# MLP third layer two periods late beside the first layer; pixels and channels turned in 64-row tiles

## The chip, the cores and the metric

One Trainium2 chip, one of its cores. The metric is the device time in microseconds (us) of one execution. The engines are called PE (TensorE), DVE (VectorE), ACT (ScalarE), POOL (GpSimd) and SP (SyncE, which here only issues DMAs).

## The reference

Two layers run over x of shape 8 x 512 x 32 x 32, that is 8 images of 512 channels and 1024 pixels.

```python
x = x + _L0_conv_ref(_gn(x), ...)   # group norm, 8-head attention over 1024 pixels, output projection
x = x + _L1_conv_ref(_gn(x), ...)   # windowed deformable attention, below
```

The second layer normalises over channels, cuts the image into 16 windows of 8 x 8 pixels and, for each of 8 groups of 64 channels, finds 4 sample points in a window, takes keys and values there, and lets each pixel attend to the 4 points of its window. To the similarities a bias is added, made by a small MLP from the distance of pixel and point:

```python
mu = x.mean(axis=1, keepdims=True)
xn = (x - mu) / jnp.sqrt(var + 1e-06) * ln_w[None, :, None, None] + ln_b[None, :, None, None]
q = jnp.einsum('bgihw,goi->bgohw', xg, wq)
...
bias = jnp.sign(pos) * jnp.log1p(jnp.abs(pos))        # 2 numbers per pair of pixel and point
bias = jax.nn.relu(bias @ cpb_w1.T + cpb_b1)          # 2 -> 128, the first layer
bias = jax.nn.relu(bias @ cpb_w2.T + cpb_b2)          # 128 -> 128, the second layer
bias = bias @ cpb_w3.T + cpb_b3                       # 128 -> 1, the third layer
```

The MLP runs over 8 groups x 16 windows x 4 points x 64 pixels per image.

## The kernel before, in words

**Order.** Each engine has its own program, with the order written out by hand and semaphores between the engines. The loop runs over the images i = 0..7. An image's turn is 32 steps of attention (first layer of the reference), the output projection (L603), the group norm and the windowing of the result, and then the **MLP stage**: `mlp(i - 1, i)` computes the MLP of the image before, and beside it the channel norm of image i. The MLP of image 7 runs alone at the end (`i is None`). So there are 8 MLPs; 7 of them carry the norm of an image. Image 0 has its norm without an MLP.

**The MLP.** It has 32 units (u = 0..31) in 16 pairs (v = 0..15). For a unit, PE makes the first layer with two matmuls over tiles of 32 rows (`mlp1_unit`, L833; a pair gives four matmuls that run beside each other). ACT takes the relu as the high half (`relu1`, L1118), DVE the low half (`low1`, L1567). The second layer is three matmuls of 128 x 128 x 512 for each half unit (`mlp2(u, w)`, L852 to L854, into three banks that go round). ACT empties one half unit of each unit (L1134), DVE the other (L1583), into `H2`, a ring of 4 units. The third layer (`mlp3(v)`, L862) takes a pair of units in tiles of 32 columns, 8 instructions, all summed into one bank `OB`. The PE order of one pair, here called a period, is written out in L884 to L891:

```python
for v in range(1, WIN):
    if v + 1 < WIN:
        mlp1(v + 1)
    mlp2(2 * v, 0)
    mlp2(2 * v, 1)
    mlp2(2 * v + 1, 0)
    mlp3(v - 1)
    mlp2(2 * v + 1, 1)
```

`mlp1(v + 1)` waits until DVE has emptied both first-layer slots; `mlp2(u, 0)` waits for `low1(u)`; each `mlp2` waits until the bank of three half units earlier is empty; ACT and DVE wait with unit u until `mlp3` of the units in its ring place is done.

**The norm beside it.** At the MLP's start PE turns the normalised image from channel rows to pixel rows (`pixels(n)`, n = 0..3, L806, 8 transposes of 128 x 128 each, two banks per n; n even is emptied by ACT at L1124, n odd by DVE at L1437). DVE takes statistics of the 8 pixel tiles (`row_stats`, L1444) after units 0 to 7, their means after unit 9 (`row_means`, L1448 to L1452) and the shifts after unit 12; ACT normalises the 8 tiles in place (L1107) after units 14 to 21. At the end PE turns them back (`channel(t)`, t = 0..3, L817, 8 transposes each): `channel(0)` stands between the last second layer and `mlp3(15)`, the other three behind it. Channel tiles are emptied with the affine scale: t = 0, 2 by DVE (`affine`, L1461), t = 1, 3 by ACT (L1272), out of two slots in turn. Then follow the transposes of the bias (L901) and `queries` (L825, 16 matmuls). For image 0 the same operations use the ring slots (L1260 and L1763 empty the pixels).

**A DMA beside it.** Before the stage, `point_outputs` are kept by ACT in a place that the high halves of units 2 and 3 share. So `relu1(2)` waits (`ms_out`) until SP's DMA has taken them to DRAM.

**Elsewhere.** The attention turns its exponentials with transposes of 64 rows (`turn`, L660: 16 of them, the two row halves into two banks), and L1079 and L1398 empty these with a pattern that puts the halves together.

## Time and profile before

| what | us |
|---|---|
| median of 3 runs | 3103.03 |
| lowest, highest | 3098.18, 3104.87 |
| the profiled execution's own time | 3095.78 |
| its span, first to last instruction | 3094.0 |

The page gives, for each engine, its busy time and share of the span, and the chain of work that ended last. The mean granted clock of PE was 0.966 of full. In the timelines each line is a start, a duration, an engine, a line of the kernel, the operation and its tiles, and in brackets the idle time of the engine before it and what ended that. A matmul's duration includes its passage through the array, so the cost of one in a stream is read from start to start.

### The profile page before, as it was taken

Reading aid. Unit: us, or ns where it says so; the run is one execution under the profiler, and the core shown is the slowest. Engines: PE = TensorE matmul, PEld = TensorE weight load, DVE = VectorE, ACT = ScalarE, POOL = GpSimd, SP = SyncE. Lnnn points to the kernel's source line nnn. Section 1 sums busy time; section 2 is a strip of 40 time slices with the busy share of each in tenths; the row PEclk is TensorE's granted clock in tenths of the full one; section 3 lists DMA queues with packets and bytes.
Section 4 is the critical chain, followed back from the end, with each engine's and each line's share of the span. In section 5 each row is a group of like instructions: output and inputs, shape, how many; then the busy total and the mean of one; then the engine's idle time right before and its main releaser. Section 6 shows DMA issues by size and latency. Waiting matters only on the chain.

```text
span 3094.0 us, 59663 instructions
## 1 busy us (share of the span) xinstructions
PE 2826.2 (91%) x24696; PEld 1964.6 (63%) x24696; DVE 2207.2 (71%) x2934; ACT 1657.7 (54%) x2429; POOL 197.0 (6%) x157
## 2 busy tenths in 40 slices
PE   6999799999999999899999999999998999998858
PEld 5666576756766577665776667665676756765434
DVE  5666677687775787767867777668777587775746
ACT  2563465374663755535654556536465375663624
POOL 0000020000200002000020001100020000200200
PEclk9999899999999999999999999999999999998968
DMA  5123013311134011340123211332113311104040
GB/s 196 51 59 110 28 33 90 116 58 52 37 80 165 6 54 37 102 145 28 37 62 119 93 42 32 64 123 79 44 38 86 121 51 52 37 12 169 14 105 28
DMA packets 141534, 221.10 MB, mean 71 GB/s; under 512 B 77713, under 2 KB 96660, under 8 KB 137396
## 3 DMA queue, kind: packets, MB, share of 16 engines
q1 hardware_dynamic: 136596, 190.03, 19.8%
q10 hardware_dynamic: 4672, 27.26, 3.6%
q8 instruction: 199, 3.26, 0.7%
q14 instruction: 67, 0.55, 0.1%
HBM read 162.40 MB, written 54.84 MB: 70 GB/s over the span
## 4 chain that ended last, share of the span: by engine, by line
PE 71%; DVE 16%; issue 4%; DMA 3%; ACT 3%; SPq 1%; another core or an unknown queue 0%; ACTq 0%; DVEq 0%; POOL 0%
PE banks L673 12%; PE banks L613 10%; PE banks L642 9%; PE banks L660 8%; PE banks L603 6%; PE banks L852 5%; PE banks L715 4%; PE banks L862 3%; DVE neg_max L1389 3%; PE banks L853 3%; PE banks L854 3%; DVE exps_turned L1398 3%; DMA point_outputs_dram<-point_outputs 2%; PE banks L825 2%; DVE qk_halves L1567 1%
## 5 line engine op out<-in xcount | busy, mean ns | idle before, releaser
L1389 DVE TENSOR_REDUCE neg_max<-banks 128x1 f32<-128x1024 f32 x512 | 601.4, 1216 | 91.1 <-PE banks L642 90.3
L1069 ACT ACTIVATE exps<-banks,neg_max 128x1024 f32<-128x1024 f32 x512 | 566.6, 1113 | 46.7 <-DVE neg_max L1389 46.5
L1079 ACT ACTIVATE exps_turned<-banks 128x1024 f32<-128x1024 f32 x256 | 262.3, 1025 | 579.8 <-PE banks L660 569.4
L1398 DVE COPY exps_turned<-banks 128x1024 f32<-128x1024 f32 x256 | 313.1, 1223 | 324.7 <-PE banks L660 310.5
L642 PE MATMUL banks<-qk_halves 64*128 64x512 f32 x3072 | 440.3, 418 | 72.1 <-ACT exps L1069 49.2
L673 PE MATMUL banks<-exps_turned,values 128*64 128x256 f32 x4096 | 480.0, 384 | 0.8 <-issue 0.8
L660 PEld LDWEIGHTS banks<-ident,exps 64*128 64x128 f32 x8192 | 312.1, 140 | 215.4 <-issue 190.1
L660 PE MATMUL banks<-ident,exps 64*128 64x64 f32 x8192 | 367.4, 229 | 43.8 <-DVE exps_turned L1398 38.7
L642 PEld LDWEIGHTS banks<-qk_halves 64*128 64x128 f32 x3072 | 296.9, 192 | 124.4 <-issue 88.7
L673 PEld LDWEIGHTS banks<-exps_turned,values 128*64 128x64 f32 x4096 | 279.7, 137 | 138.3 <-issue 4.0
L1567 DVE SCALAR_TENSOR_TENSOR qk_halves<-banks,qk_halves 128x1024 fp32r<-128x1024 f32 x256 | 301.6, 1217 | 85.6 <-ACT qk_halves L1118 85.4
L613 PE MATMUL banks<-x_hi,wqk_ring 128*128 128x512 f32 x992 | 340.0, 406 | 0.0
L1118 ACT ACTIVATE qk_halves<-banks 128x1024 fp32r<-128x1024 f32 x256 | 249.2, 1023 | 147.5 <-PE banks L833 128.2
L852 PE MATMUL banks<-qk_halves,mlp_w_hi 128*128 128x512 f32 x512 | 233.1, 455 | 28.4 <-ACT exps L1134 21.6
L613 PEld LDWEIGHTS banks<-x_hi,wqk_ring 128*128 128x128 f32 x992 | 188.5, 190 | 44.5
L1583 DVE TENSOR_SCALAR exps<-banks,mlp_b 128x512 f32<-128x512 f32 x256 | 189.9, 745 | 31.9 <-PE banks L854 24.8
L852 PEld LDWEIGHTS banks<-qk_halves,mlp_w_hi 128*128 128x128 f32 x512 | 98.3, 192 | 177.3 <-ACT exps L1134 125.6
L853 PE MATMUL banks<-qk_halves,mlp_w_hi 128*128 128x512 f32 x512 | 205.2, 401 | 0.0
L854 PE MATMUL banks<-qk_halves,mlp_w_lo 128*128 128x512 f32 x512 | 204.3, 399 | 0.0
L613 PE MATMUL banks<-x_lo,wqk_ring 128*128 128x512 f32 x496 | 195.5, 394 | 0.0
L715 PE MATMUL banks<-wv_halves,x_hi 128*128 128x512 f32 x512 | 168.8, 411 | 18.4 <-DVE x_lo L1360 18.4
L1134 ACT ACTIVATE exps<-banks,mlp_b 128x512 f32<-128x512 f32 x256 | 168.4, 693 | 28.9 <-PE banks L854 28.4
(181 smaller groups left out, 3344.2 us busy)
## 6 DMA issues: line engine op xcount, KB each, us to landing
wqk_ring<-wqk_split SPq DMA_DIRECT2D x62, 512.0 KB, 4.3
wo_halves<-wo_split_dram SPq DMA_DIRECT2D x8, 2048.0 KB, 7.6
exps_turned<-in_x SPq DMA_DIRECT2D x32, 512.0 KB, 5.5
x_dram<-exps SPq DMA_DIRECT2D x32, 512.0 KB, 2.6
exps_turned<-x_dram SPq DMA_DIRECT2D x32, 512.0 KB, 6.2
out<-exps_turned SPq DMA_DIRECT2D x32, 512.0 KB, 2.8
recips_b<-recips_dram SPq DMA_DIRECT2D x240, 64.0 KB, 3.5
x_image<-in_x ACTq DMA_DIRECT2D x14, 1024.0 KB, 14.2
```

What stands on the lines that cost most here:

```text
L613: mm = pe.matmul(dst, weights[:, a, k], half[:, k, c:c + 512], start=(k == 0 and a == 0 and half is XH), stop=(k == CT - 1 and a == 1))
L642: mm = pe.matmul(slot(("s", 2 * n + h, i))[:, 512 * c:512 * c + 512], QK[rows, p % 2, a, P * j:P * j + P], QK[rows, p % 2, b, 512 * c:512 ...
L660: mm = pe.transpose(TB[:, r, kt * D:kt * D + D], PB[rows, 2 * h + n % 2, kt * P:(kt + 1) * P], IDENT[rows, rows])
L673: mm = pe.matmul(OB[D * h:D * h + D, 0:256], V[:, kt, hc:hc + D], PT[:, u % 2, h, kt], start=(kt == 0), stop=(kt == KT - 1))
L715: mm = pe.matmul(slot(("v", n, i))[:, 512 * s:512 * s + 512], half[:, k, P * tt:P * tt + P], WV[:, a, k], start=(k == 0 and half is XH and ...
L852: pe.matmul(h2_bank(c), W2H[:], h1_hi_half(u)[:, cols], start=True, stop=False)
L853: pe.matmul(h2_bank(c), W2H[:], h1_lo_half(u)[:, cols], start=False, stop=False)
L854: pe.matmul(h2_bank(c), W2L[:], h1_hi_half(u)[:, cols], start=False, stop=True)\
L1069: freed(act.activation(PB[:, 2 * h + n % 2], slot(("s", m, i)), ACT.Exp, bias=NM[:, m:m + 1], accum_out=SS[:, m:m + 1]), ("s", m, i))
L1389: dve.tensor_reduce(NM[:, m:m + 1], slot(("s", m, i)), AX.X, ALU.max, negate=True).then_inc(mx, 1)
L1398: dve.tensor_copy(PT[:, n // 2 % 2, 1, :, P * j:P * j + P].rearrange("p k (r q) -> p k r q", r=2), TB.rearrange("p r (k q) -> p k r q", k= ...
L1567: freed(dve.scalar_tensor_tensor(out=h1_lo_half(u), in0=slot(("h1", u, j)), scalar=0.0, in1=h1_hi_half(u).bitcast(F32), op0=ALU.max, op1=A ...
```

## The change

The third layer now comes two periods late: `mlp3(v - 2)` directly behind `mlp1(v + 1)`, ahead of the four `mlp2` of the period, which follow each other without a break. `mlp3(14)` stands behind the last `mlp2`, ahead of `channel(0)`. For that, `H2` becomes a ring of 6 units: the two new ones, `H2X`, lie in free space behind `window_outputs`. DVE's statistics go from units 0 to 7 to the even units 0 to 14, the means to unit 16 and the shifts to unit 18, ACT's normalising to units 21 to 28. The transposes of pixels and channels are made as 16 of 64 rows in place of 8 of 128 rows, the upper and lower row halves into two banks, and the six lines that empty them put the halves together by their access pattern. No instruction is added or removed on ACT, DVE, POOL or SP.

```diff
+        H2X = at("mlp_hidden_more", [P, 2, HW], AT_PT + 8192)
...
+        def h2_unit(u):
+            return H2[:, u % 6] if u % 6 < 4 else H2X[:, u % 6 - 4]
+
+        def pixel_halves(ap):
+            return ap.rearrange("p b (t r c) -> p (b t) r c", t=CT, r=2)
+
+        def from_halves(ap):
+            return ap.rearrange("p (r x c) -> p x r c", r=2, c=D)
+
+        def channel_halves(t):
+            return A[:, t].rearrange("p (x r c) -> p x r c", r=2, c=D)
...
@@ pixels(n, i), 8 of 128 rows become 16 of 64 rows
-                        mm = pe.transpose(dst[:, 512 * s + P * t:512 * s + P * (t + 1)],
-                                          A[:, t, P * (2 * n + s):P * (2 * n + s + 1)], IDENT[:])
+                        for r in range(2):
+                            rows = slice(D * r, D * r + D)
+                            c0 = 512 * r + D * (CT * s + t)
+                            mm = pe.transpose(dst[:, c0:c0 + D], A[rows, t, P * (2 * n + s):P * (2 * n + s + 1)],
+                                              IDENT[rows, rows])
@@ channel(t, i)
-                    mm = pe.transpose(slot(("tc", t, i))[:, P * r:P * (r + 1)], XP[:, r, P * t:P * (t + 1)], IDENT[:])
+                    for h in range(2):
+                        rows = slice(D * h, D * h + D)
+                        c0 = 512 * h + D * r
+                        mm = pe.transpose(slot(("tc", t, i))[:, c0:c0 + D], XP[rows, r, P * t:P * (t + 1)],
+                                          IDENT[rows, rows])
@@ mlp3(v)
-                                       H2[:, (2 * v + s // 2) % 4, 512 * (s % 2):512 * (s % 2) + 512],
+                                       h2_unit(2 * v + s // 2)[:, 512 * (s % 2):512 * (s % 2) + 512],
@@ mlp(j, i), PE
-                    mlp2(2 * v, 0)
-                    mlp2(2 * v, 1)
-                    mlp2(2 * v + 1, 0)
-                    mlp3(v - 1)
-                    mlp2(2 * v + 1, 1)
+                    if v >= 2:
+                        mlp3(v - 2)
+                    for u in (2 * v, 2 * v + 1):
+                        for w in range(2):
+                            mlp2(u, w)
+                mlp3(WIN - 2)
                 if i is not None:
                     channel(0, i)
                 mlp3(WIN - 1)
@@ mlp(j, i), ACT
-                        act.activation(XP[:, 4 * n:4 * n + 2].rearrange("p b c -> p (b c)"), TB_ALL,
+                        act.activation(pixel_halves(XP[:, 4 * n:4 * n + 2]), from_halves(TB_ALL),
...
-                    if u >= 4:
-                        act.wait_ge(l3_done, j * WIN + u // 2 - 1)
-                    act.activation(H2[:, u % 4, 0:512], h2_bank(2 * u), ACT.Relu, bias=B2[:, 0:1])\
+                    if u >= 6:
+                        act.wait_ge(l3_done, j * WIN + u // 2 - 2)
+                    act.activation(h2_unit(u)[:, 0:512], h2_bank(2 * u), ACT.Relu, bias=B2[:, 0:1])\
                         .then_inc(h2_done[0], 1)
-                    if i is not None and 14 <= u < 22:
-                        normalise_rows(u - 14, i)
+                    if i is not None and 21 <= u < 29:
+                        normalise_rows(u - 21, i)
@@ mlp(j, i), DVE: the ring's waits as on ACT, and
-                        if u < PXT:
-                            ins = row_stats(u, i)
-                            if u == PXT - 1:
+                        if u < 2 * PXT and u % 2 == 0:
+                            ins = row_stats(u // 2, i)
+                            if u == 2 * PXT - 2:
                                 after = mark(ins)
-                        if u == PXT + 1:
+                        if u == 2 * PXT:
                             row_means(after)
-                        if u == PXT + 4:
+                        if u == 2 * PXT + 2:
                             row_shifts(i)
```

The other lines that empty pixels (L1260, L1437, L1763) and channels (L1272, L1461) get the same patterns.

## Rows read from the trace of the kernel before

**Rows 1.** The page, its parts 1 and 4: engines, and the chain by engine.

```profile
PE 2826.2 (91%) x24696; PEld 1964.6 (63%) x24696; DVE 2207.2 (71%) x2934; ACT 1657.7 (54%) x2429; POOL 197.0 (6%) x157
...
PE 71%; DVE 16%; issue 4%; DMA 3%; ACT 3%; SPq 1%; another core or an unknown queue 0%; ACTq 0%; DVEq 0%; POOL 0%
```

**Rows 2.** Timeline of PE, one period (start us, duration us, ..., [idle before <-releaser]).

```profile
1051.52 0.39 PE L833 MATMUL banks<-attended,mlp_w_rows 21*128 21x512 bf16 x4
1051.85 0.50 PE L852 MATMUL banks<-qk_halves,mlp_w_hi 128*128 128x512 f32 x1
1052.18 0.40 PE L853 MATMUL banks<-qk_halves,mlp_w_hi 128*128 128x512 f32 x1
...
1053.79 0.39 PE L854 MATMUL banks<-qk_halves,mlp_w_lo 128*128 128x512 f32 x1
1054.11 1.07 PE L862 MATMUL banks<-exps,mlp_w_slide 128*32 128x512 f32 x8
1055.11 0.50 PE L852 MATMUL banks<-qk_halves,mlp_w_hi 128*128 128x512 f32 x1
...
1056.00 0.39 PE L833 MATMUL banks<-attended,mlp_w_rows 21*128 21x512 bf16 x4
```

**Rows 3.** The same timeline, DVE, the same period.

```profile
1053.01 2.36 DVE L1567 SCALAR_TENSOR_TENSOR qk_halves<-banks,qk_halves 128x1024 fp32r<-128x1024 f32 x2 [0.63 <-ACT qk_halves L1118]
```

**Rows 4.** Timeline of DVE where it never stops, earlier in this MLP.

```profile
1016.68 0.68 DVE L1444 BATCH_NORM_STATS2 ln_bn<-pixels 128x6 f32<-128x512 f32 x1
1017.28 2.34 DVE L1567 SCALAR_TENSOR_TENSOR qk_halves<-banks,qk_halves 128x1024 fp32r<-128x1024 f32 x2
1019.53 1.41 DVE L1583 TENSOR_SCALAR exps<-banks,mlp_b 128x512 f32<-128x512 f32 x2
1020.86 0.18 DVE L1450 BATCH_NORM_AGGREGATE ln_mean_var<-ln_bn 128x2 f32<-128x6 f32 x1
```

**Rows 5.** Timeline of ACT in a period with two L1107 rows.

```profile
1038.47 1.94 ACT L1118 ACTIVATE qk_halves<-banks 128x1024 fp32r<-128x1024 f32 x2
```

**Rows 6.** Timeline of PE: starts of L833 in three periods following each other.

```profile
1015.20 0.39 PE L833 MATMUL banks<-attended,mlp_w_rows 21*128 21x512 bf16 x4
...
1019.82 0.40 PE L833 MATMUL banks<-attended,mlp_w_rows 21*128 21x512 bf16 x4
...
1024.59 0.40 PE L833 MATMUL banks<-attended,mlp_w_rows 21*128 21x512 bf16 x4
```

**Rows 7.** Timeline of PE at the end of the last MLP.

```profile
3069.56 1.07 PE L862 MATMUL banks<-exps,mlp_w_slide 128*32 128x512 f32 x8 [0.94 <-DVE exps L1583]
```

**Rows 8.** Timeline of PE in the attention: transposes of 64 rows, and what follows.

```profile
1110.87 0.71 PE L660 MATMUL banks<-ident,exps 64*128 64x64 f32 x16
1111.39 0.94 PE L642 MATMUL banks<-qk_halves 64*128 64x512 f32 x6
```

**Rows 9.** Timeline of the channel stage behind an MLP.

```profile
1069.16 1.04 PE L817 MATMUL banks<-ident,pixels 128*128 128x128 f32 x8
...
1072.38 1.20 ACT L1272 ACTIVATE normed<-banks,ln_b_T,ln_w_T 128x1024 f32<-128x1024 f32 x1 [0.32 <-PE banks L817]
...
1073.73 1.07 PE L817 MATMUL banks<-ident,pixels 128*128 128x128 f32 x8 [0.51 <-ACT normed L1272]
...
1075.07 1.45 PE L825 MATMUL banks<-normed,wq_blocks 128*128 128x512 f32 x3
```

**Rows 10.** The page, part 5: the copy out of two banks with a pattern.

```profile
L1079 ACT ACTIVATE exps_turned<-banks 128x1024 f32<-128x1024 f32 x256 | 262.3, 1025 | 579.8 <-PE banks L660 569.4
```

**Rows 11.** Waits of L1118 (ACT): until, us in total, times.

```profile
  DMA point_outputs_dram<-point_outputs: 19.1, 5
```

**Rows 12.** Timeline of the first image: its channel stage.

```profile
338.83 6.37 PE L817 MATMUL banks<-ident,pixels 128*128 128x128 f32 x32 [6.15 <-DVE qk_halves L1373]
```

**Rows 13.** Windows: length, busy of PE PEld DVE ACT POOL, PEclk, DMA, GB/s.

```profile
1071.30:1075.10 3.80, 3.29 (x32) 3.08 (x30) 1.62 (x2) 2.15 (x3) 0.00 (x0) 1.00 0.00 0
...
999.70:1002.70 3.00, 3.00 (x10) 1.60 (x9) 3.00 (x5) 1.50 (x3) 0.00 (x0) 0.50 0.83 333
```

More of the change, by code:

```diff
@@ L1259, in _ @@
                     wait_full(act, ("tp", n, i))
-                    freed(act.activation(XP[:, 2 * n:2 * n + 2].rearrange("p b c -> p (b c)"), slot(("tp", n, i)),
+                    freed(act.activation(pixel_halves(XP[:, 2 * n:2 * n + 2]), from_halves(slot(("tp", n, i))),
                                          ACT.Copy), ("tp", n, i))
@@ L1271, in _ @@
                     wait_full(act, ("tc", t, i))
-                    freed(act.activation(A[:, t], slot(("tc", t, i)), ACT.Identity, scale=LNWT[:, t:t + 1],
+                    freed(act.activation(channel_halves(t), from_halves(slot(("tc", t, i))), ACT.Identity, scale=LNWT[:, t:t + 1],
                                          bias=LNBT[:, t:t + 1]), ("tc", t, i))
@@ L1436, in pixel_rows @@
                 dve.wait_ge(tpx_full[1], 2 * (i - 1) + n // 2 + 1)
-                dve.tensor_copy(XP[:, 2 * n:2 * n + 2].rearrange("p b c -> p (b c)"), OM_ALL).then_inc(tpx_done[1], 1)
+                dve.tensor_copy(pixel_halves(XP[:, 2 * n:2 * n + 2]), from_halves(OM_ALL)).then_inc(tpx_done[1], 1)
             def row_stats(r, i):
@@ L1460, in affine @@
                 wait_full(dve, ("tc", t, i))
-                freed(dve.tensor_scalar(A[:, t], slot(("tc", t, i)), LNWT[:, t:t + 1], LNBT[:, t:t + 1], ALU.mult, ALU.add),
+                freed(dve.tensor_scalar(channel_halves(t), from_halves(slot(("tc", t, i))), LNWT[:, t:t + 1],
+                                        LNBT[:, t:t + 1], ALU.mult, ALU.add),
                       ("tc", t, i))
@@ L1580, in mlp @@
                     dve.wait_ge(h2_full[1], j * UNITS + u + 1)
-                    if u >= 4:
-                        dve.wait_ge(l3_done, j * WIN + u // 2 - 1)
-                    dve.tensor_scalar(H2[:, u % 4, 512:1024], h2_bank(2 * u + 1), B2[:, 0:1], 0.0, ALU.add, ALU.max)\
+                    if u >= 6:
+                        dve.wait_ge(l3_done, j * WIN + u // 2 - 2)
+                    dve.tensor_scalar(h2_unit(u)[:, 512:1024], h2_bank(2 * u + 1), B2[:, 0:1], 0.0, ALU.add, ALU.max)\
                         .then_inc(h2_done[1], 1)
                     if i is not None:
-                        if u < PXT:
-                            ins = row_stats(u, i)
-                            if u == PXT - 1:
+                        if u < 2 * PXT and u % 2 == 0:
+                            ins = row_stats(u // 2, i)
+                            if u == 2 * PXT - 2:
                                 after = mark(ins)
-                        if u == PXT + 1:
+                        if u == 2 * PXT:
                             row_means(after)
-                        if u == PXT + 4:
+                        if u == 2 * PXT + 2:
                             row_shifts(i)
@@ L1762, in _ @@
                         wait_full(dve, ("tp", n, i))
-                        freed(dve.tensor_copy(XP[:, 2 * n:2 * n + 2].rearrange("p b c -> p (b c)"),
-                                              slot(("tp", n, i))), ("tp", n, i))
+                        freed(dve.tensor_copy(pixel_halves(XP[:, 2 * n:2 * n + 2]),
+                                              from_halves(slot(("tp", n, i)))), ("tp", n, i))
                 if i:
```

## The prediction

> **What bounds the kernel now.** I read the page first: PE is busy for 91% of the span and the chain that ended last runs over PE for 71% and over DVE for 16% [rows 1]. So what counts is time on PE, and the places where PE waits for an emptying engine. Then I read one period of the MLP on PE's timeline [rows 2]. From L833 to the next L833 it is 4.48 us, and PE has no idle time in it. To be seen are the steps from start to start. Inside a run of second-layer matmuls a step is 0.23 (seven of them from 1052.18 to 1053.79). The first matmul of 128 rows behind a tiled block takes 0.33, the last one before a tiled block 0.32, L833 to what follows 0.33, and L862 to what follows 1.00. So each tiled block costs about 0.10 in front and 0.10 behind beyond its own work, and a period has two such blocks. In this period DVE sits idle for 0.63, until ACT's high half is there [rows 3]: PE sets the pace, DVE follows.
>
> **The third layer beside the first.** The new period on PE is L833, L862, then twelve matmuls: 0.33 + 1.00 + 0.33 + 10 x 0.23 + 0.32 = 4.28, that is 0.20 less than 4.48 [rows 2]. This takes the step from the first layer (row tiles) to the third (column tiles) at 0.33, as the step from the first layer to the second; no row shows it. The bounds: it costs nothing (0.10 less) or 0.20 more, so that nothing is gained. I take the middle, since every switch in the rows costs about 0.10. Blocks that merge: v = 2 to 14, 13 per MLP, 8 MLPs: 13 x 8 x 0.20 = **20.8 us**. At v = 15 `mlp3(13)` stands alone as before; `mlp3(14)` no longer splits a run of matmuls, which spares one long first step, 0.1 x 8 = **0.8**. In the last MLP, PE waits 0.94 for DVE ahead of `mlp3(15)` [rows 7]; `mlp3(14)` now fills that: **0.9**.
>
> The Trainium skill, page "TensorEngine Tiling (Array Packing)", section "Key Properties", says that a change of the tiling mode, not of the tile alone, drains the engine. By this the step from first to third layer is a switch as well and the sum stays; without a drain there it would be the 0.10 less per merged block of the first rival. The rows agree for full and tiled blocks (0.10 on each side).
>
> Does anything else stop a period of 4.28? DVE's load with one `row_stats` is 0.60 + 2.25 + 1.33 = 4.18 [rows 4]. Its first `low1` starts 1.49 after L833 [rows 2, 3]; 1.49 + 4.18 = 5.67, and the next may start at 4.28 + 1.49 = 5.77. It fits by 0.10. ACT with two L1107 per period has no idle time at 4.48 [rows 5], so its load is up to 0.20 over the new period, for three periods and one half at each side. That backlog of at most 0.6 first eats the slack of the first-layer slots: DVE's second `low1` ends 1.49 + 2.36 = 3.85 after L833, 0.43 ahead of where PE asks [rows 2, 3]. I take 0 and keep 0.2 x 7 = 1.4 as bound. The waits on the longer ring ask for a third layer two periods old; nothing queues behind them.
>
> **Statistics spread.** Two `row_stats` per period put DVE behind, and the periods after them take 4.62 and 4.77 [rows 6]; over 4.48 that is 0.43. Spread out, DVE keeps up; the means come where no statistics are left. I take 0.3 x 7 = **2.1** (bounds 0 and 3.0). The shifts and the normalising come seven units later; unit 28 is two periods ahead of `channel(0)`, which waits for them: nothing.
>
> **Transposes.** Eight of 128 rows with the four of L901 take 1.34, or 0.11 each, 0.89 for eight [rows 9]. Sixteen of 64 rows that turn as much take 0.52, from 1110.87 to the next start [rows 8]. So one group saves up to 0.4. That the halves run beside each other is shown there, with the same operands.
> In the channel stage: `channel(0)` is ahead of `mlp3(15)` on PE, 0.4. ACT's affine waits 0.32 for `channel(1)`, and then `channel(3)` waits for that affine [rows 9]: shorter transposes take off the 0.32, after which ACT itself is late (its bias row stands ahead). `channel(3)` is shorter by 0.4 itself. With rounding 1.2 of the 4 x 0.4 arrives at `queries` at 1075.07, and behind it PE and DVE follow each other. 1.2 x 7 = **8.4** (bounds 0.4 and 1.6 each, 2.8 and 11.2).
> The emptying lines read two banks side by side. The nearest row is L1079, 1025 ns for 128x1024 [rows 10], beside two L1118 in 1.94 [rows 5]: I take 0. For the affine no row exists; 0.1 each, two on the path, is the bound, 1.4.
> In the pixel stage five of seven MLPs then wait for the DMA of the point outputs, 19.1 us together [rows 11]: what PE gains there goes into that wait. If the DMA were early, 0.4 more each, 2.0. The other two give at most 0.4 each; I take **0.5** in all. In the first image nothing hides the turning, and its 32 transposes take 6.37 [rows 12]: between 1.2 and 3.2; I take 2.0, and 0.8 for its pixels (bounds 0 and 1.6), **2.8**.
>
> **Sum.** 20.8 + 0.8 + 0.9 + 2.1 + 8.4 + 0.5 + 2.8 = 36.3, say 36 us. The profiled execution took 3095.8, so it would be 3059.8. That execution lies 7.3 under the median of 3103.0; for the median I expect **3067**.
>
> **Rivals.** A difference within 0.2% (6 us) can't be told from none here.
> 1. The switch from first to third layer is free. Then the period is 4.18, where DVE's 4.18 is the bound too: 13 x 8 x 0.10 = 10 more, 3057. Against it: no switch in the rows is free. 7%.
> 2. Merging saves nothing, because that switch costs 0.20 more; 36 - 21 = 15, so 3088. For it: row tiles to column tiles is the one switch not in these rows. This is also the case in which the change does not do what it says. 8%.
> 3. DVE becomes the bound of the eight periods with statistics. It fits by 0.10 only. If each period kept the idle 0.63 ahead of `low1` [rows 3], it would be 4.18 + 0.63 = 4.81 there, 8 x 0.53 x 7 = 30 lost, 3097. Against it: that idle time is there because PE is slower than DVE. 5%.
> 4. PE's clock. It fell to 0.50 in a stretch of 3.0 us, in which PE was busy for all of it [rows 13]; at half speed such a stretch costs 1.5. It followed a wait in the MLP's start. Shorter transposes with the same waits leave PE emptier in the channel and pixel stages. One more such stretch per norm, 7 x 1.5 = 10: 3077. Against it: in the channel stage the granted clock stays at 1.00 with 0.51 idle [rows 9, 13]. 10%.
> 5. The same, strong enough to turn the sign. It decides from 36 / 1.5 = 24 more low stretches, over three per image; with four, 42 lost, 3109: slower. 2%.
>
> On 4 and 5: from 1071.30 to 1075.10 nearly all of PE's work is transposes, and the granted clock is 1.00 [rows 13]. The Trainium skill, page "TensorE: Matmul & The Clock Gate", section "Part 4: PE-mode transpose", says that transposes do not count as work for the clock. By that rule shorter transposes could only help the clock, and 4 and 5 would have no chance. The trace disagrees with it, so I keep them.
>
> **The numbers.** The forecast has 68%, its own range with the bounds above 3058 to 3075. The range of 8 in 10 takes in rivals 1, 2 and 4: 3052 to 3088. Faster by over 0.2%: all but rival 5 and part of 3, 95%; same 3%, slower 2%.
>
> **What would show it.** On PE's timeline L833 follows L833 after 4.28, L862 stands 0.33 behind L833, and the runs of twelve have steps of 0.23; with 4.18 or 4.48 rival 1 or 2 is right. With rival 3 the periods of the even units up to 14 are longer than the later ones, with DVE named ahead of L833. The channel stage, from the last L854 to L825, is shorter by 1.2 beyond the moved third layer. Windows show the clock. The prediction is wrong if the periods stay at 4.48, or if ACT's wait for the DMA grows by more than the pixels gave.

## The result, and the profile after

| what, us | before | after |
|---|---|---|
| median, 4 runs each, on the same chip | 3102.02 | 3061.58 |
| lowest, highest | 3098.18, 3104.87 | 3059.65, 3069.95 |
| ratio of the medians, 95% interval | | 0.9876 [0.9853, 0.9898] |
| profiled execution, own time | 3095.78 | 3069.95 |
| its span | 3094.0 | 3068.1 |
| mean granted clock | 0.966 | 0.963 |

The change makes the kernel faster by 40 us (the interval of the ratio is 32 to 46). The execution that was profiled is the slowest of the four of after, 8.4 over the median; its span is only 25.9 shorter than before's. So the traces must be read by stages, and something in this execution gives back a part of the gain. The page first, to compare with [rows 1]:

```profile
PE 2788.4 (91%) x25208; PEld 1956.1 (64%) x25208; DVE 2200.3 (72%) x2934; ACT 1667.9 (54%) x2429; POOL 196.7 (6%) x157
...
PE 74%; DVE 13%; DMA 5%; issue 3%; ACT 3%; SPq 2%; another core or an unknown queue 0%; ACTq 0%; DVEq 0%; POOL 0%
```

PE's busy time went down by 38 and its share of the chain up, at DVE's cost (16% to 13%). The DMA's share went from 3% to 5%: there stands a part of what was given back. The timeline of PE in one period, the answer to [rows 2] (L853 is the first layer, L872 to L874 the second, L882 the third; L1139, L1155, L1128 on ACT are the old L1118, L1134, L1107, and L1589 on DVE the old L1567):

```profile
1033.67 0.39 PE L853 MATMUL banks<-attended,mlp_w_rows 21*128 21x512 bf16 x4
1033.99 1.06 PE L882 MATMUL banks<-mlp_hidden_more,mlp_w_slide 128*32 128x512 f32 x8
1034.99 0.50 PE L872 MATMUL banks<-qk_halves,mlp_w_hi 128*128 128x512 f32 x1
1035.32 0.39 PE L873 MATMUL banks<-qk_halves,mlp_w_hi 128*128 128x512 f32 x1
...
1037.62 0.39 PE L874 MATMUL banks<-qk_halves,mlp_w_lo 128*128 128x512 f32 x1
1037.94 0.39 PE L853 MATMUL banks<-attended,mlp_w_rows 21*128 21x512 bf16 x4
```

L882 stands 0.32 behind L853, then come 1.00, 0.33, ten steps of 0.23 and 0.32: a period is 4.27, and PE never waits. DVE where it has one `row_stats` per period, the answer to [rows 4]:

```profile
1016.07 0.74 DVE L1605 TENSOR_SCALAR mlp_hidden_more<-banks,mlp_b 128x512 f32<-128x512 f32 x1
1016.73 0.68 DVE L1465 BATCH_NORM_STATS2 ln_bn<-pixels 128x6 f32<-128x512 f32 x1
1017.33 0.74 DVE L1605 TENSOR_SCALAR mlp_hidden_more<-banks,mlp_b 128x512 f32<-128x512 f32 x1
1018.07 1.23 DVE L1589 SCALAR_TENSOR_TENSOR qk_halves<-banks,qk_halves 128x1024 fp32r<-128x1024 f32 x1
```

The profile names no idle time here, but the next L853 on PE does not wait for it. From its start the first L1605 takes 0.66 to the next row and the second 0.74; the 0.08 more may be what DVE has left over in a period. ACT in the periods with two L1128, the answer to [rows 5]:

```profile
1038.65 1.93 ACT L1139 ACTIVATE qk_halves<-banks 128x1024 fp32r<-128x1024 f32 x2
...
1043.01 1.95 ACT L1139 ACTIVATE qk_halves<-banks 128x1024 fp32r<-128x1024 f32 x2
...
1047.38 1.98 ACT L1139 ACTIVATE qk_halves<-banks 128x1024 fp32r<-128x1024 f32 x2
```

These are 4.36 and 4.37 apart, with no idle time between: here ACT is the bound. PE's L853 starts at 1042.21, 1046.59 and 1050.97, so two periods of an MLP take 4.38. The channel stage, the answer to [rows 9]:

```profile
1060.20 0.71 PE L836 MATMUL banks<-ident,pixels 64*128 64x64 f32 x16
...
1060.84 1.06 PE L882 MATMUL banks<-exps,mlp_w_slide 128*32 128x512 f32 x8
...
1061.84 1.32 PE L836 MATMUL banks<-ident,pixels 64*128 64x64 f32 x32
...
1062.60 1.20 ACT L1293 ACTIVATE normed<-banks,ln_b_T,ln_w_T 128x1024 f32<-128x1024 f32 x1
...
1063.94 0.71 PE L836 MATMUL banks<-ident,pixels 64*128 64x64 f32 x16 [0.78 <-ACT normed L1293]
...
1065.08 1.45 PE L845 MATMUL banks<-normed,wq_blocks 128*128 128x512 f32 x3
```

From the last third layer, L882 at 1060.84, to the queries at L845 it is 4.24, where before it was 4.81 (L862 to L825, 1075.07). The affine at 1062.60 has no idle time in front of it, where [rows 9] had 0.32; `channel(3)` now waits 0.78 for it instead of 0.51. The block of 16 transposes at 1060.20 takes 0.64 to the next start, where 8 of 128 rows took 1.10 (1069.16 to 1070.26). The end of the last MLP, the answer to [rows 7], and the first image's channel stage, the answer to [rows 12]:

```profile
3042.78 0.39 PE L874 MATMUL banks<-qk_halves,mlp_w_lo 128*128 128x512 f32 x1
3043.10 1.07 PE L882 MATMUL banks<-mlp_hidden_more,mlp_w_slide 128*32 128x512 f32 x8
3044.11 1.06 PE L882 MATMUL banks<-exps,mlp_w_slide 128*32 128x512 f32 x8
3045.97 0.66 PE L922 MATMUL banks<-ident,exps 128*128 128x128 f32 x4 [0.80 <-ACT exps L1162]
```

```profile
334.99 2.31 PE L836 MATMUL banks<-ident,pixels 64*128 64x64 f32 x32 [5.96 <-DVE qk_halves L1394]
337.63 2.17 PE L836 MATMUL banks<-ident,pixels 64*128 64x64 f32 x32 [0.34 <-DVE normed L1482]
340.19 2.08 PE L845 MATMUL banks<-normed,wq_blocks 128*128 128x512 f32 x2 [0.39 <-DVE normed L1482]
```

The 0.94 of waiting is gone: `mlp3(14)` fills it. The last place is the MLP's start. The waits of L1139, the answer to [rows 11], and one of them in the timeline:

```profile
  DMA point_outputs_dram<-point_outputs: 35.9, 7
```

```profile
989.81 1.94 ACT L1139 ACTIVATE qk_halves<-banks 128x1024 fp32r<-128x1024 f32 x2 [5.95 <-DMA point_outputs_dram<-point_outputs]
...
992.38 0.80 PE L872 MATMUL banks<-qk_halves,mlp_w_hi 128*128 128x512 f32 x1 [5.29 <-ACT exps L1155]
...
992.98 0.63 PE L873 MATMUL banks<-qk_halves,mlp_w_hi 128*128 128x512 f32 x1
...
993.40 0.63 PE L874 MATMUL banks<-qk_halves,mlp_w_lo 128*128 128x512 f32 x1
```

All seven MLPs wait there now, for 35.9 in all, where before five waited 19.1. PE runs out of work behind it for 5.29, and its next steps are 0.42 instead of 0.23 (992.98 to 993.40). Last, windows of the channel stage and of this start, the answer to [rows 13]:

```profile
1061.00:1064.70 3.70, 2.92 (x57) 1.90 (x50) 2.65 (x2) 1.83 (x3) 0.00 (x0) 1.00 0.00 0
988.70:998.80 10.10, 6.42 (x17) 4.36 (x18) 7.40 (x9) 5.66 (x8) 0.00 (x0) 0.50 0.78 275
```

The granted clock stays at 1.00 in the channel stage, though PE is busy there for only 2.92 of 3.70. It falls to 0.50 while PE stands idle in the wait for the DMA (its last matmul before is at 986.70), and stays there for the 10.1 us of the second window.

A table by stages shows the whole. It is worked out from the starts of PE's rows in the timeline and summed over the MLPs. The **start** runs from the first L833 (now L853) to that of pair 1, and the **wait** from there to that of pair 2, the stretch with the DMA wait. The **periods** run to `mlp3(15)` and the **channels** from there to the queries. The last MLP is counted apart, and so is the first image, from its projection to its queries. "Low" is the time at the low clock (granted 0.50), over the whole span.

| us | before | after | forecast of the difference |
|---|---|---|---|
| start, 7 MLPs | 51.7 | 51.1 | -0.5 |
| wait, 7 MLPs | 37.7 | 49.5 | 0 |
| periods, 7 MLPs | 488.2 | 464.3 | -23.8 (18.2 + 0.7 + 2.1, and 0.4 x 7 of the channels) |
| channels, 7 MLPs | 33.7 | 29.6 | -5.6 (the other 0.8 x 7) |
| last MLP and its tail | 103.9 | 99.4 | -3.6 (2.6 + 0.1 + 0.9) |
| first image | 65.4 | 63.0 | -2.8 |
| low | 210 | 230 | |

Without the row of the wait the differences make 35.3 (from the unrounded starts), against a forecast of 36.3. The wait gives back 11.8, and the remaining 2.4 of the 25.9 lie outside these stages. Two rows hide something. The start is 0.28 shorter in six MLPs (6.61 to 6.33) and 1.03 longer in the seventh (12.07 to 13.10), which stays unexplained. And the wait costs more than its own row: the first period behind it, from pair 2 to pair 3, is counted in the periods, and its mean granted clock is 0.55 to 0.78 in after, where it was 0.73 to 1.00 in before.

### The profile page after: what moved, and what is told of

It reads as the page before. It is cut to its first block, busy times and chain, and to the rows that moved or that the text cites. A ratio compares the mean times of both kernels' runs of the same rounds, so it can differ in the third digit from the quotient of the medians.

```text
span 3068.1 us, 60655 instructions
## 1 busy us (share of the span) xinstructions
PE 2788.4 (91%) x25208; PEld 1956.1 (64%) x25208; DVE 2200.3 (72%) x2934; ACT 1667.9 (54%) x2429; POOL 196.7 (6%) x157
## 4 chain that ended last, share of the span: by engine, by line
PE 74%; DVE 13%; DMA 5%; issue 3%; ACT 3%; SPq 2%; another core or an unknown queue 0%; ACTq 0%; DVEq 0%; POOL 0%
PE banks L686 12%; PE banks L626 10%; PE banks L655 9%; PE banks L673 9%; PE banks L616 6%; PE banks L872 5%; PE banks L882 4%; PE banks L873 4%; PE banks L874 4%; PE banks L728 4%; DMA point_outputs_dram<-point_outputs 3%; DVE neg_max L1410 3%; DVE exps_turned L1419 3%; PE banks L845 2%; SPq L487 2%
## 5 line engine op out<-in xcount | busy, mean ns | idle before, releaser
L1090 ACT ACTIVATE exps<-banks,neg_max 128x1024 f32<-128x1024 f32 x512 | 566.9, 1114 | 46.2 <-DVE neg_max L1410 46.0
L1589 DVE SCALAR_TENSOR_TENSOR qk_halves<-banks,qk_halves 128x1024 fp32r<-128x1024 f32 x256 | 302.1, 1220 | 89.0 <-ACT qk_halves L1139 88.7
L1139 ACT ACTIVATE qk_halves<-banks 128x1024 fp32r<-128x1024 f32 x256 | 249.7, 1029 | 77.4 <-PE banks L853 41.6
L872 PE MATMUL banks<-qk_halves,mlp_w_hi 128*128 128x512 f32 x512 | 224.5, 438 | 34.0 <-ACT exps L1155 31.6
L873 PE MATMUL banks<-qk_halves,mlp_w_hi 128*128 128x512 f32 x512 | 206.9, 404 | 0.0
L874 PE MATMUL banks<-qk_halves,mlp_w_lo 128*128 128x512 f32 x512 | 206.6, 403 | 0.0
L872 PEld LDWEIGHTS banks<-qk_halves,mlp_w_hi 128*128 128x128 f32 x512 | 100.2, 196 | 157.2 <-issue 99.7
L616 PE MATMUL banks<-attended_hi,wo_halves 128*128 128x512 f32 x512 | 160.0, 394 | 5.5 <-DMA wo_halves<-wo_split_dram 5.5
L1155 ACT ACTIVATE exps<-banks,mlp_b 128x512 f32<-128x512 f32 x176 | 121.8, 698 | 62.8 <-PE banks L874 62.8
## 6 DMA issues: line engine op xcount, KB each, us to landing
x_image<-in_x ACTq DMA_DIRECT2D x14, 1024.0 KB, 10.6
```

The lines of the kernel that those rows point to most:

```text
L616: mm = pe.matmul(dst[:, 512 * n:512 * n + 512], weights[:, a, k, n0:n0 + P], half[:, k, 512 * n:512 * n + 512], start=(k == 0 and a == 0 a ...
L872: pe.matmul(h2_bank(c), W2H[:], h1_hi_half(u)[:, cols], start=True, stop=False)
L873: pe.matmul(h2_bank(c), W2H[:], h1_lo_half(u)[:, cols], start=False, stop=False)
L874: pe.matmul(h2_bank(c), W2L[:], h1_hi_half(u)[:, cols], start=False, stop=True)\
L1090: freed(act.activation(PB[:, 2 * h + n % 2], slot(("s", m, i)), ACT.Exp, bias=NM[:, m:m + 1], accum_out=SS[:, m:m + 1]), ("s", m, i))
L1589: freed(dve.scalar_tensor_tensor(out=h1_lo_half(u), in0=slot(("h1", u, j)), scalar=0.0, in1=h1_hi_half(u).bitcast(F32), op0=ALU.max, op1=A ...
```

## The experiments

All ratios are to the kernel before, run beside the variant on the same chip. Three chips were used. The medians of before on them were 3119.97 (`t_only`, `m_only`, `split3`, `ms_moved`), 3124.42 (`after_again`, `before_ms`, `stats_packed`, `paired3`) and 3107.66 (`ms_again`, `ms_early1`, `pix128`, `ch128`), so the kernels are compared by ratio, and a ratio is turned into microseconds with the median of its chip. Each profile is one execution.

### 1. One half of the change at a time

`t_only` is the kernel before with only the 64-row transposes and the six patterns (the hunks `pixels` and `channel` of the diff, L1260, L1437, L1763, L1272, L1461, L1124). `m_only` is the change without these.

> The kernel before with only the transposes in 64 rows; the MLP's order, ring and statistics stay. If the terms of the sum add up, it is faster than before by 8.4 (channel) + 0.5 (pixels) + 2.8 (first image) = 12 us, ratio 0.996. Rival: the pixels' part goes into the wait for the point outputs' DMA and the channel stage gives only what the trace after shows from mlp3(15) to the queries (4.34 to 3.76, 0.6 per image, and 0.5 ahead of it): then 5 to 8 us. MLP periods stay at 4.48 in both.

> The changed kernel with its transposes put back to 128 rows: only the third layer's place, the ring of six and the spread statistics are left. Theory (terms add): 20.8 + 0.8 + 0.9 + 2.1 = 25 us faster than before, ratio 0.992, periods 4.27. Rival (the transposes carry more than their term, or the DMA wait eats part of this one): under 18 or over 32 us.

Measured: `t_only` 3111.28, 0.9968 [0.9951, 0.9984], a gain of 10. `m_only` 3097.97, 0.9934 [0.9912, 0.9957], a gain of 21. The stages say why neither is larger. In `t_only` the start gains 0.28 in six of the seven MLPs and the channels 0.58 in each; but the wait takes 44.2 where before took 37.7, and the periods 492.6 where before took 488.2. All of the latter is the first period behind the wait: its seven add up to 44.5 against 39.4, at a mean granted clock of 0.62 to 0.75. In `m_only` the periods and the last MLP gain 20.1 and 5.0, which is the expected 25, and the wait gives back 8.5. The two gains add up to 31; with intervals of 5 to 15 and of 13 to 27 that doesn't contradict the 40 of the whole. The interval of `t_only` takes in both its expectation (12) and most of its rival (5 to 8), so the times don't decide between them.

### 2. The third layer late, but not beside the first

Is it the merging that gains, or only that the third layer comes late and the second layer is never waited for? `split3` keeps the six-unit ring and the lateness, and puts the tiled block back where it was:

```diff
-                    if v >= 2:
-                        mlp3(v - 2)
-                    for u in (2 * v, 2 * v + 1):
-                        for w in range(2):
-                            mlp2(u, w)
+                    mlp2(2 * v, 0)
+                    mlp2(2 * v, 1)
+                    mlp2(2 * v + 1, 0)
+                    if v >= 2:
+                        mlp3(v - 2)
+                    mlp2(2 * v + 1, 1)
```

> The changed kernel with the third layer, still two periods late, put back between the third and the fourth second-layer product, away from the first layer. Theory (a tiled block of its own costs 0.10 in front and 0.10 behind): periods go from 4.27 to 4.48, 13 x 8 x 0.2 = 21 us slower than the changed kernel, so 19 us faster than before. Rival (the gain comes from waiting less for the emptying of H2, since the third layer asks for older data, not from merged blocks): periods stay at 4.3 and it is as fast as the changed kernel, 40 us faster than before.

Measured: 3107.25, 0.9960 [0.9944, 0.9975], a gain of 12 (8 to 17) where the whole change has about 40 and 19 were expected. The timeline of PE in one period:

```profile
1063.30 0.40 PE L853 MATMUL banks<-attended,mlp_w_rows 21*128 21x512 bf16 x4
1063.63 0.50 PE L872 MATMUL banks<-qk_halves,mlp_w_hi 128*128 128x512 f32 x1
...
1065.58 0.39 PE L874 MATMUL banks<-qk_halves,mlp_w_lo 128*128 128x512 f32 x1
1065.90 1.06 PE L882 MATMUL banks<-exps,mlp_w_slide 128*32 128x512 f32 x8
1066.90 0.50 PE L872 MATMUL banks<-qk_halves,mlp_w_hi 128*128 128x512 f32 x1
...
1067.79 0.39 PE L853 MATMUL banks<-attended,mlp_w_rows 21*128 21x512 bf16 x4
```

The step from L853 to a full block (0.33), the step into L882 (0.32) and that out of it (1.00 for 8 matmuls) are all as in [rows 2], and the period is 4.49 again; the periods' stage takes 485.2, against 464.3 in after and 466.0 in its repetition (section 3). So the gain is the pair of transitions that the merged block does without. The lateness by itself brings nothing that shows: the periods are 3.0 shorter than in before, and the spread statistics account for that (3.4, see the part on the prediction). The 7 us by which the expectation missed have their like in the wait, whose stage takes 43.9 where before took 37.7.

### 3. The statistics as they were

```diff
-                        if u < 2 * PXT and u % 2 == 0:
-                            ins = row_stats(u // 2, i)
-                            if u == 2 * PXT - 2:
+                        if u < PXT:
+                            ins = row_stats(u, i)
+                            if u == PXT - 1:
@@ the means at PXT + 1 and the shifts at PXT + 4, as before
```

> The changed kernel itself, for its trace a second time and to compare with the others of this call. Theory: 37 to 41 us faster than before, ratio 0.987 to 0.988; the wait of ACT for the point outputs' DMA (35.9 us in the first trace) is the part that moves from execution to execution. Rival: that wait is the same each time, within 3 us.

> The changed kernel with DVE's statistics back behind units 0 to 7, the means behind unit 9, the shifts behind unit 12. Theory (the spread was worth its term): the periods behind the statistics go to 4.6 or more, 2 to 4 us slower than the changed kernel. Rival (at periods of 4.27 a DVE load of 4.8 bites fully, eight units in four periods at 4.8): 4 x 0.5 x 7 = 14 us slower. Second rival: no difference, the early MLP waits anyway.

Measured: `after_again` (the changed kernel once more) 3085.43, 0.9869 [0.9849, 0.9889]; `stats_packed` 3093.10, 0.9905 [0.9892, 0.9918]. Packed statistics cost 8 us by the medians and 11 by the ratios. My expectation of 2 to 4 fell, and the rival's 14 was too much. The periods' stage takes 472.6, against 466.0 in `after_again` and 464.3 in after, 0.9 to 1.2 more per MLP. The six periods from pair 3 to pair 9, where nearly all of the packed statistics stand, are together 7.5 longer in the seven MLPs than in after. PE's timeline, with two `row_stats` per period on DVE:

```profile
2121.79 0.40 PE L853 MATMUL banks<-attended,mlp_w_rows 21*128 21x512 bf16 x4 [0.29 <-DVE qk_halves L1589]
...
2126.55 0.40 PE L853 MATMUL banks<-attended,mlp_w_rows 21*128 21x512 bf16 x4 [0.42 <-DVE qk_halves L1589]
```

These periods are 4.76 long and PE names DVE's L1589 ahead of L853. That is the same length as the worst of before [rows 6]: with two `row_stats` in each period DVE becomes the bound once its slack is used up, whatever PE would do, and in such periods all that the shorter one could bring is lost. The prediction had measured the spread against a period of 4.48; against one of 4.28 it is worth 0.2 more for each such period, and for those in which DVE catches up.

### 4. The wait for the point outputs

`ms_moved` is the change with the point outputs kept elsewhere, in the place of units 4 and 5 of the ring, so that `relu1(2)` waits for nothing; the wait moves to unit 4. `before_ms` moves them to the same place in the kernel before, where no unit of the ring lies, and there the wait stands only ahead of DVE's first copy of turned exponentials of the next image. (`ms_moved` has this wait too, once, in image 1.) And `ms_again` is `ms_moved` once more.

```diff
-        MS = at("point_outputs", [P, CT, C], AT_QK + 24576)
+        MS = at("point_outputs", [P, CT, C], AT_PT + 8192)
...
-                    if u == 2:
-                        act.wait_ge(ms_out, 16 * (j + 2))
@@ ahead of the emptying into unit 4, on ACT and on DVE
+                    if u == 4:
+                        act.wait_ge(ms_out, 16 * (j + 2))
```

> The changed kernel with the buffer of the point outputs moved from the place shared with the high halves of units 2 and 3 into the place of the two new ring units, so that ACT asks for the DMA's landing with unit 4 and not with unit 2. In the trace after, ACT waits for that DMA in all seven MLPs, 35.9 us together. Theory (that wait is on the path since the pixel stage got shorter): from L833 of pair 1 to that of pair 2 it goes from 5.8 to 8.2 down to 4.3, in sum 10 to 20 us faster than the changed kernel. Rival (the rows of the MLP or the emptying engines end next at nearly the same time, or the low clock follows all the same): within 4 us of the changed kernel.

> The kernel before with only the buffer of the point outputs moved to the free place behind window_outputs, and the wait of relu1(2) for it gone; a wait at the next image's first copy guards the buffer. In the trace before, ACT waits 19.1 us for that DMA in five MLPs. Theory (the DMA was on the path in part already): 8 to 14 us faster than before, less than the 14 us between the changed kernel and the same move there. Rival (the wait is new with the change, and before it was covered): within 3 us of before.

> The kernel with the moved buffer a second time, as the base of the next one on the same chip: 50 to 56 us faster than before, ratio 0.982 to 0.984; from L853 of pair 1 to that of pair 2 it takes 4.1 to 4.5 in all seven MLPs with a norm. If instead it is near 0.987, the gain of the move in the first call was chance.

Measured: `ms_moved` 3067.66, 0.9830 [0.9807, 0.9854]; `before_ms` 3107.45, 0.9949 [0.9934, 0.9964]; `ms_again` 3048.67, 0.9823 [0.9803, 0.9843]. In all three no engine waits for this DMA any more, and the stage of the wait takes 29.6 to 30.2, where before takes 37.7 and the two profiles of after 49.5 and 43.9. So the wait was on the path before the change: to take it away is worth 16 there (11 to 21). The stage of the wait explains 7.5 of it in the two profiles; that of before has less waiting than those of the changed kernel, and no second one was taken. In the changed kernel it is worth 12 to 16 (0.9876 and 0.9869 against 0.9830 and 0.9823). Without the wait the change itself is worth 53 - 16 = 37 us, give or take 9 by the two intervals.

The timeline of ACT and PE shows what is left at this place in `ms_moved`:

```profile
995.95 1.94 ACT L1137 ACTIVATE qk_halves<-banks 128x1024 fp32r<-128x1024 f32 x2 [2.43 <-PE banks L853]
...
998.52 0.50 PE L872 MATMUL banks<-qk_halves,mlp_w_hi 128*128 128x512 f32 x1 [1.77 <-ACT exps L1155]
```

ACT now waits 2.43 for PE, because the first layer of pair 1 stands behind six second-layer matmuls, and PE then waits 1.77 for ACT.

### 5. The transposes' places one by one

`pix128` is after with only the pixels turned in 128 rows, `ch128` with only the channels. Each was run once.

> The changed kernel with the pixels alone turned in 128 rows. For its stages only: from the first L853 of an MLP to that of pair 1 it takes 6.6 as before and not 6.3, while the channel stage stays short (3.76 from the last third layer to the queries). Rival (the halves of the channels do the pixels' part too): 6.3.

> The changed kernel with the channels alone turned in 128 rows. From the last third layer to the queries 4.34 as before and not 3.76, and from the third layer of pair 14 to that of pair 15 about 2.1 and not 1.64; the pixel stage stays at 6.3. By the prediction's term the two differences come to 1.2 us per image; the traces so far say 0.58 + 0.43 = 1.0.

Measured: 3055.39 and 3059.50, beside a median of before of 3107.66. One execution each can't rank them, so only their stages are read. Channels: `ch128` takes 33.7 for the channels, as before, and `pix128` 29.6, as after. From the third layer of pair 14 to that of pair 15, with `channel(0)` between, `ch128` takes 2.02 and `pix128` 1.64. A row of `ch128`, as in [rows 9]:

```profile
1065.60 1.07 PE L833 MATMUL banks<-ident,pixels 128*128 128x128 f32 x8 [0.51 <-ACT normed L1289]
```

First image: neither 65.40 (before), pixels alone (`ch128`) 64.69, channels alone (`pix128`) 63.75, both 63.04. By these the pixels are worth 0.71 and the channels 1.65. But two more kernels with neither took 64.60 (`before_ms`) and 64.52 (`m_only`), less than the one with the pixels alone; so the channels are worth 0.8 to 1.65, and a gain of the pixels is shown only beside short channels. Pixels beside an MLP: in `pix128` the start is longer by 1.6 for six MLPs, but the wait takes 39.0 against 49.5 and 43.9, with 4 waits for the DMA of 17.2 in all. That what the pixels gain in front of that wait goes into it is not shown by this: `m_only` has the same pixels, and its wait takes 46.2.

### 6. Two attempts to gain more

`paired3` is `ms_moved` with two third layers behind each other in every other period, so that a step from the first to the third layer and one from the third to the second are spared there.

```diff
-                    if v >= 2:
-                        mlp3(v - 2)
+                    if v % 2 == 0:
+                        if v >= 4:
+                            mlp3(v - 3)
+                        mlp3(v - 2)
...
+                mlp3(WIN - 3)
                 mlp3(WIN - 2)
```

> The kernel with the moved buffer, and two third layers made one behind the other in every second period (even v: pairs v-3 and v-2), so that the odd periods have one tiled block less. Theory (a switch from first to third layer costs about 0.10, whole blocks are what counts): the odd periods lose 1.0 of the third layer and its switch, two periods together take 8.45 and not 8.55, 6 x 8 x 0.10 = 5 us faster than the moved buffer alone, 58 us faster than before. Rival (DVE's or ACT's load of 4.2 to 4.4 per period bounds the odd periods, which are shorter): no gain or 1 to 4 us slower.

Measured: 3102.81, 0.9934 [0.9919, 0.9949], 32 us slower than `ms_moved` by the ratios. The expectation fell, and the rival, which named the cause, had at most 4. The timeline of one odd period and the start of the even one (PE, ACT and DVE):

```profile
1043.26 0.39 PE L853 MATMUL banks<-attended,mlp_w_rows 21*128 21x512 bf16 x4
...
1043.69 1.94 ACT L1140 ACTIVATE qk_halves<-banks 128x1024 fp32r<-128x1024 f32 x2 [0.32 <-PE banks L853]
...
1044.75 2.36 DVE L1594 SCALAR_TENSOR_TENSOR qk_halves<-banks,qk_halves 128x1024 fp32r<-128x1024 f32 x2 [0.50 <-ACT qk_halves L1140]
...
1046.26 0.50 PE L872 MATMUL banks<-qk_halves,mlp_w_hi 128*128 128x512 f32 x1 [0.32 <-ACT exps L1158]
...
1047.25 0.40 PE L853 MATMUL banks<-attended,mlp_w_rows 21*128 21x512 bf16 x4
...
1047.58 1.06 PE L882 MATMUL banks<-exps,mlp_w_slide 128*32 128x512 f32 x8
...
1048.46 1.04 PE L882 MATMUL banks<-mlp_hidden_more,mlp_w_slide 128*32 128x512 f32 x8
...
1049.43 0.50 PE L872 MATMUL banks<-qk_halves,mlp_w_hi 128*128 128x512 f32 x1
```

The period without a third layer needs 3.3 on PE (4.27 less the block) but takes 3.99. The chain behind it reads off these rows: L853 at 1043.26, ACT's high half at 1043.69, DVE's `low1` at 1044.75 for 2.36, which ends at 1047.11, and PE can write the slots again at 1047.25. In between PE waits 0.32 for ACT's L1158 besides. This is the 3.85 of the prediction (1.49 + 2.36, [rows 2, 3]) as a floor for a period, whatever PE has to do. The even periods have two third layers and take 5.13 to 5.17. Together that is 9.1 for two periods, against 8.55.

`ms_early1` is `ms_moved` with the first layer of pair 1 ahead of the second layer of unit 0, which is what section 4 showed to be late, and with the normalising spread so that at most every other period has two L1128.

```diff
+                mlp1(1)
                 mlp2(0, 0)
                 mlp2(0, 1)
-                mlp1(1)
...
-                    if i is not None and 21 <= u < 29:
-                        normalise_rows(u - 21, i)
+                    if i is not None and u in (20, 21, 23, 24, 26, 27, 29, 30):
+                        normalise_rows((20, 21, 23, 24, 26, 27, 29, 30).index(u), i)
```

> The moved buffer, and PE makes the first layer of pair 1 ahead of the second layer of unit 0, right behind the pixels; ACT normalises behind units 20, 21, 23, 24, 26, 27, 29 and 30. In the trace of the moved buffer ACT idles 2.43 us for that first layer, and PE then waits 1.77 for ACT; the two last periods take 4.38. Theory: relu1(2) starts 1.1 to 1.4 us earlier per MLP, 8 to 10 us, and 1.5 us from the last periods: 10 us faster than the moved buffer, ratio 0.979 to 0.980. Rival (the wait for the first-layer slots, which DVE frees, ends at nearly the same time, or the low clock takes it back): within 3 us of the moved buffer.

Measured: 3039.94, 0.9786 [0.9770, 0.9801], 0.0037 or 11.5 us below `ms_again` (8.7 by the medians), as expected, and the fastest version of this study: 26 to 28 us below the changed kernel (0.9876 and 0.9869). The same place as above:

```profile
987.23 0.40 PE L853 MATMUL banks<-attended,mlp_w_rows 21*128 21x512 bf16 x4 [0.42 <-DVE qk_halves L1591]
...
987.72 1.94 ACT L1137 ACTIVATE qk_halves<-banks 128x1024 fp32r<-128x1024 f32 x2 [1.33 <-PE banks L853]
...
992.09 0.39 PE L853 MATMUL banks<-attended,mlp_w_rows 21*128 21x512 bf16 x4
```

ACT's wait is 1.33 instead of 2.43, and behind L853 PE has no idle time. The start takes 1.1 less per MLP (5.2 against 6.3), and the last periods are back at 4.27. L853 at 987.23 now waits 0.42 for DVE's L1591, ahead of which DVE copied pixels (984.74, for 1.21): DVE is what is late next.

## Why the prediction was right

The time was forecast at 3067 and is 3061.6, inside the likeliest case's own range of 3058 to 3075. The mechanism of the largest term is shown. That the sum by stages came within 1 us (35.3 for 36.3) is partly luck: the statistics and the last MLP gave more than their terms, the channels, ACT and the first image less. And one of the prediction's own signs of being wrong came true in the profile, the growth of the wait. Point by point:

- **The third layer beside the first, 20.8 + 0.8 + 0.9.** Right. The step of 0.33 that no row showed is 0.32, the period 4.27 for the 4.28 forecast. The twelve periods from pair 3 to pair 15 are 18.0 shorter in the seven MLPs, once the statistics' 3.4 and ACT's 1.5 (below) are taken out, which is 0.21 for each. The last MLP with its tail gave 4.4 for the 3.6 expected. `split3` shows that the order is the cause. Rivals 1 (a period of 4.18) and 2 (4.48) fell by this one row.
- **DVE fits by 0.10.** Right, and it was this tight: the profile names no idle time of DVE with one `row_stats`, the period is still 4.27, and rival 3 fell. `stats_packed` shows the other side of the edge, 4.76.
- **Statistics spread, 2.1.** Too small, and over its bound of 3.0. In before the six periods from pair 3 to pair 9 are longer than six of 4.485 by 1.1 in the first MLP and by 0.35 to 0.40 in each other one, 3.4 in all; in after they are six times 4.27. The first MLP is the one in which the period behind the wait ran at a granted clock of 1.00 and not of 0.73 to 0.83; there four of these periods and not two are long, up to 4.80, which [rows 6], taken from another MLP, could not show. And this counts only what was better than before; the part without which the merging would not have paid in the first half of each MLP is 8 to 11 us by the times, 7.5 by these periods.
- **ACT with two L1128, taken as 0 with a bound of 1.4.** It came to the bound: 2 periods x 0.11 x 7 MLPs = 1.5. The slack did absorb the first of it: L1139 starts 0.43 behind L853 at 1033.67, and 0.71, 0.80 and 0.79 behind it in the next three. With that it was used up, and PE took ACT's pace.
- **Channels, 8.4.** Mis-sized too: 0.46 at `channel(0)` (0.64 for 1.10) and 0.57 behind `mlp3(15)`, 7.2 in all. With the third layers in the same places, in `ch128`, `channel(0)` is worth only 0.38. The affine's 0.32 went, as forecast. But `channel(3)` is shorter only by 0.26: from 1063.94 to L922 at 1064.59 it takes 0.65, where 128 rows took 0.91 (1073.73 to L901 at 1074.64). In [rows 8] sixteen transposes of 64 rows took 0.52, with another block of 64-row tiles behind them; here full tiles follow, and the change costs 0.13. The transposes of 128 rows needed no change there. The prediction had counted changes of tiling for the MLP and not for the transposes.
- **First image, 2.8.** 2.4 against the profile of before, and 1.5 against the two other kernels with 128-row transposes. The channels gave 0.8 to 1.65 for 2.0; the pixels' 0.8 is not shown.
- **Pixels, 0.5, and the wait for the DMA.** The start is 0.6 shorter in all. The wait was seen, its size was not, and the prediction's last sign of being wrong came true in the profile: ACT's wait for the DMA grew from 19.1 to 35.9, far more than the pixels gave. This is not what the pixels gained: `m_only` has the pixels of before and waits 31.7. Over the runs with the wait in place it was 17.2 to 35.9, also for kernels with the same start. The DMA is issued at the same place, 5.7 to 5.8 ahead of the first L833 or L853 in most MLPs, but the median time from issue to landing is 12.4 and 12.6 in the two profiles with the least waiting (`pix128` 17.2, before 19.1), 13.1 to 13.9 in the five between (25.7 to 31.4), and 14.3 and 14.6 in those with the most (`m_only` 31.7, after 35.9). So the DMA itself takes longer in some executions; what makes it take longer wasn't settled. The medians say that it costs about as much in the kernel before (16) as in the changed one (12 to 16), and so it moved the profile, not the result: 37 for the change without it, 36 forecast.
- **The clock, rivals 4 and 5.** Half seen. The low time grew from 210 to 230, but not where I expected it: the channel stage keeps 1.00. It grew in the starts of the seven MLPs, from 31 to 58 in sum, in four of them from a stretch of 3.4 to one of 6.8 to 10.2 behind the wait for the DMA, and in the first image's channel stage, from 6.8 to 10.2. Elsewhere it fell. Without the wait it is 198 to 218, in `ms_early1` 192. So much of it follows the waits, but not all: in `ms_early1` the clock is at 0.50 from 987.8 to 991.2, though the waits of PE just before were 0.20, 0.77 and 0.42. It turned no sign.

Two things were measured that the rows of before could not say. A change from row tiles to column tiles costs like one from or to the full array (L853 to L882 is 0.32). And two column-tiled blocks behind each other cost nothing between them: in `paired3` the first takes 0.88 to the second (1047.58 to 1048.46), the second 0.97 to the full tiles behind it. The 1.01 from 3043.10 to 3044.11 in the last MLP does not contradict this, since DVE's last emptying ends only at 3043.96. The Trainium skill, page "TensorEngine Tiling (Array Packing)", section "Key Properties", says that the change of mode is what drains, and not the change of the tile. The trace agrees with it in both, and in the 0.13 behind `channel(3)`.

## What to carry to other kernels

Where a stretch of PE changes its tiling often, count the changes from start to start and put the tiled blocks beside each other: here a change costs 0.10 at each side, and a deeper ring pays for the lateness. Before a period is shortened, add up each other engine's load in it, instruction by instruction, and find the chain that frees its buffers; the work that was bunched in the old period has to be spread first, and under the floor of that chain (3.99 here) nothing more is gained. A wait that a profile shows only in some of the stages is worth an experiment of its own: a buffer placed elsewhere gave 12 to 16 us, a third as much as the whole change.

## What was not expected of the hardware

- The DMA that takes the point outputs away took 10.6 to 15.9 from issue to landing in the MLPs with a norm, and the waits for it added up to 17.2 to 35.9 in kernels with nearly the same start. Their share of the medians was 12 to 16.
- In after PE stands idle for 3.0 to 6.4 us behind that wait, and in six of the seven MLPs it comes back at the low of its two clocks (0.50, 1.2 GHz), where a step takes 0.42 instead of 0.23; in the other, after 3.4 us, it comes back at 1.00. Such a wait costs more than its length.
- Reading the two banks with a pattern of halves cost nothing that shows: the affine with it takes 1.20 on ACT, as before [rows 9], and 1.34 on DVE, as before; DVE's copy of the pixels takes 1.22 in both.
